# An attention block with its softmax maximum subtracted on VectorE, and three reorderings around it, on one core

## The reference

```python
x = x + tanh(g_xattn) * attention(layernorm(x), ctx, pos, Wq, Wkv, Wout, bout)   # 32 heads of 16
x = x + tanh(g_ffn)   * ffn(layernorm(x), gate_w, w1, w2, shared_w1, shared_w2)

# attention: q = rope(x @ Wq), k = rope(ctx @ Wk), v = ctx @ Wv
#            softmax(q k^T / 4) v, then @ Wout + bout
# ffn:       softmax over 16 experts, the best 6 of each token,
#            each expert and a shared one: (silu(x w1g) * (x w1u)) w2
```

## Time and profile before

| | us |
|---|---|
| median of 3 runs (1628.78 to 1642.08) | 1639.48 |
| the profiled execution | 1645.52 |
| its span, first to last instruction | 1643.7 |
| PE busy (matmul) | 1531.2 |
| DVE busy | 674.6 |
| ACT busy | 563.9 |
| POOL busy | 674.2 |

### The profile page before, as it was taken

One profiled execution on the slowest core, in us unless ns is written; L12 is line 12 of the kernel. 1 busy time (PEld: TensorE's weight loads), 2 busy tenths in 40 slices (PEclk: granted clock), 3 DMA queues, 4 the chain that ended last, 5 costly groups with the idle time before them and its releaser, 6 DMA issues.

```text
span 1643.7 us, 32751 instructions
## 1 busy us (share of the span) xinstructions
PE 1531.2 (93%) x9026; PEld 1296.5 (79%) x9027; DVE 674.6 (41%) x1527; ACT 563.9 (34%) x1370; POOL 674.2 (41%) x1135
## 2 busy tenths in 40 slices
PE   3997999999999873999999999999999999899998
PEld 2675667676666652999999999999999999788887
DVE  4466655555655442222222222222222222245555
ACT  3454555555554520222222222222222222211111
POOL 4436644343444223327344444444444400744442
PEclk9798979888877865999999999999999999999999
DMA  4102332221222114333333333333333232355553
GB/s 174 70 30 69 126 98 104 68 68 68 78 101 85 60 65 172 132 130 130 131 131 134 132 132 135 131 130 130 131 130 115 94 135 81 112 187 173 173 173 116
DMA packets 76313, 190.56 MB, mean 116 GB/s; under 512 B 10497, under 2 KB 12546, under 8 KB 73570
## 3 DMA queue, kind: packets, MB, share of 16 engines
q1 hardware_dynamic: 54562, 99.81, 18.7%
q0 software_dynamic: 21696, 90.06, 15.6%
HBM read 117.07 MB, written 72.76 MB: 115 GB/s over the span
## 4 chain that ended last, share of the span: by engine, by line
PE 57%; issue 1%; DVE 1%; another core or an unknown queue 1%; POOL 1%; DMA 0%; ACT 0%; SPq 0%; DVEq 0%
PE bank L1334 33%; PE bank L1364 18%; PE bank L1305 3%; PE bank L1345 3%; POOL w_lo L209 0%; DVE tree L1429 0%; POOL w_hi L205 0%; DMA xr<-expert_rows 0%; DVE comb L1434 0%; DVE tree L1431 0%; DVE tree L1432 0%; ACT silu L1277 0%; DVE x_lo L1402 0%; DVE a_lo L1408 0%
## 5 line engine op out<-in xcount | busy, mean ns | idle before, releaser
L1334 PE MATMUL bank<-w_hi,x_hi 128*128 (+1 forms) x1152 | 291.7, 334 | 1.6 <-POOL w_lo L209 1.6
L1334 PE MATMUL bank<-w_hi,x_lo 128*128 (+1 forms) x1152 | 279.7, 324 | 0.0
L1334 PE MATMUL bank<-w_lo,x_hi 128*128 (+1 forms) x1152 | 279.7, 324 | 0.0
L205 POOL CAST w_hi<-w_raw 128x352 fp32r<-128x352 f32 x144 | 62.5, 483 | 458.1 <-PE bank L1334 458.1
L1277 ACT ACTIVATE silu<-bank 128x352 f32<-128x352 f32 x144 | 67.0, 465 | 468.6 <-PE bank L1334 454.4
L525 ACT ACTIVATE soft<-bank,smax 128x128 f32<-128x128 f32 x512 | 146.6, 372 | 190.4 <-DVE smax L884 190.1
L1334 PEld LDWEIGHTS bank<-w_hi,x_lo 128*128 128x128 f32 x1152 | 201.6, 188 | 0.0
L1334 PEld LDWEIGHTS bank<-w_lo,x_hi 128*128 128x128 f32 x1152 | 201.6, 188 | 0.0
L1420 DVE SCALAR_TENSOR_TENSOR act<-silu,row_w,bank 128x352 f32<-128x352 f32 x112 | 65.0, 580 | 323.5 <-ACT silu L1277 306.7
L1334 PEld LDWEIGHTS bank<-w_hi,x_hi 128*128 128x128 f32 x1152 | 194.6, 189 | 1.8 <-POOL w_lo L209 1.8
L1364 PE MATMUL bank<-w_hi,a_hi 128*128 (+3 forms) x432 | 172.9, 400 | 13.3 <-DVE a_lo L1408 7.3
(11 more groups left out here) (184 smaller groups left out, 2427.2 us busy)
## 6 DMA issues: line engine op xcount, KB each, us to landing
xr<-expert_rows SPq DMA_DIRECT2D x112, 264.0 KB
y_rows<-y SPq DMA_DIRECT2D x112, 256.0 KB, 2.0
w_raw<-in_w POOLq DMA_DIRECT2D x18, 1408.0 KB, 6.9
w_raw<-in_w POOLq DMA_DIRECT2D x18, 512.0 KB, 8.0
x_sb<-in_x SPq DMA_DIRECT2D x16, 256.0 KB
x_res<-in_x SPq DMA_DIRECT2D x16, 256.0 KB
x_rows<-x SPq DMA_DIRECT2D x16, 256.0 KB
x_rows<-row SPq DMA_DIRECT2D x16, 256.0 KB
```

Source lines behind the costliest of these rows:

```text
L1334: last = nc.tensor.matmul(to[:, 0:WIDTH], xx[jt][:, d, :], w[d][half][:, cols], start=(d == 0 and xx is x_hi and w is w1_hi), stop=(d == D ...
```

## The change

- The block of part A ends without the drain of GpSimd (`no_gpsimd_drain=True`); GpSimd's program of part B begins with a wait for the 96 scatters instead.
- Softmax: DVE subtracts the four maxima from the scores, from PSUM into `soft` in SBUF (128x512, the maxima broadcast along 128 columns), in place of the multiplication of the 128x4 maxima; ACT has one exponential of 512 columns over `soft` in place, with an immediate scale, in place of four with a bias. The score bank is free once DVE has subtracted.
- Projections: V moves from unit 3 to unit 6 (behind `probs`), the transposition of k from unit 6 to unit 5 (behind `probs`); ACT's copies of k move from unit 7 to unit 5, the copy of V from unit 3 to unit 7, `c_hi` from unit 4 to 7; DVE's `c_lo` from unit 5 to 7.
- Part B: `combine` and `finish` of each shared tile stand one step later, its two results alternate between banks 5 and 4, and PE waits for the shared weights only at the first shared tile.

```diff
-        block = st.enter_context(nc.Block())
+        block = st.enter_context(nc.Block(no_gpsimd_drain=True))
...
                     act.wait_ge(shifted, b * GROUPS + u + 1)
-                    need(act, prob_mm, b * GROUPS + u - 1)
-                    for h in range(4):
-                        last = a.activation(soft[u % 2][:, h, :], bank[2 + u % 2][:, h * P:(h + 1) * P], ACT.Exp,
-                                            bias=smax[u % 2][:, h:h + 1], scale=SCALE)
-                    last.then_inc(exp_done, 1)
+                    a.activation(soft[u % 2][:], soft[u % 2][:], ACT.Exp, scale=SCALE).then_inc(exp_done, 1)
...
                     if at(PROJECT) and u == 7:
                         b, j, n = at(PROJECT)
+                        act.wait_ge(v_mm, b + 1)
+                        need(act, pv_mm, (b - 1) * GROUPS)
+                        act.wait_ge(ones_done, 2)
+                        a.activation(v_one[j][:, :, 0:HD], bank[0][:].rearrange("p (h d) -> p h d", h=HEADS),
+                                     ACT.Copy).then_inc(v_done, 1)
+                    attend(at, u)
+                    if at(PROJECT) and u == 5:
+                        b, j, n = at(PROJECT)
                         act.wait_ge(kt_mm, b + 1)
...
-                    attend(at, u)
...
-                    if at(LOAD) and u == 4:
+                    if at(LOAD) and u == 7:
...
-                    need(pe, exp_done, b * GROUPS + u - 1)
+                    need(pe, shifted, b * GROUPS + u - 1)
...
-                    need(pe, kt_done, 2 * b)
+                    need(pe, v_done, b)
...
-                if u == 3:
-                    pe.wait_ge(k_rot, 2 * (b + 1))
-                    three(bank[0][:], ct, kv_w, CC, lambda t, c: t[:, c, :], lambda w, c: w[:, c, D:2 * D])\
-                        .then_inc(v_mm, 1)
                 if u == 4:
                     pe.wait_ge(q_rope_done, b + 1)
-                    pe.wait_ge(v_done, b + 1)
+                    pe.wait_ge(k_rot, 2 * (b + 1))
                     four_transposes(bank[0], q_rope).then_inc(qt_mm, 1)
-                if u == 6:
+
+            def project_late(u, b, j, n):
+                if u == 5:
                     pe.wait_ge(k_rope_done, b + 1)
                     pe.wait_ge(qt_done, b + 1)
                     four_transposes(bank[0], k_rope).then_inc(kt_mm, 1)
+                if u == 6:
+                    pe.wait_ge(kt_done, 2 * (b + 1))
+                    three(bank[0][:], ct, kv_w, CC, lambda t, c: t[:, c, :], lambda w, c: w[:, c, D:2 * D])\
+                        .then_inc(v_mm, 1)
...
-                if u == 5:
+                if u == 7:
                     dve.wait_ge(c_hi_done, b + 1)
...
-                need(dve, exp_done, b * GROUPS + u - 1)
                 v.tensor_reduce(smax[u % 2][:], s3, AX.X, ALU.max).then_inc(smax_done, 1)
                 dve.wait_ge(smax_done, b * GROUPS + u + 1)
-                v.tensor_scalar(smax[u % 2][:], smax[u % 2][:], -SCALE, None, ALU.mult).then_inc(shifted, 1)
+                need(dve, prob_mm, b * GROUPS + u - 1)
+                v.tensor_tensor(soft[u % 2][:], s3, smax[u % 2][:, :, None].to_broadcast([P, 4, P]), ALU.subtract)\
+                    .then_inc(shifted, 1)
...
+        y_banks = (bank[5], bank[4])
...
+        finish_at = {min(BLOCKS + SHARED * (b + 1) + 2, STEPS + 1): b for b in range(BATCHES)}
...
+            for k in range(2):
+                pool.wait_ge(scattered[k], 16 * TOPK * BATCHES // 2)
...
-                    pe.wait_ge(w1_made, 8 * (EXPERTS + s + 1))
+                    if t == BLOCKS:
+                        pe.wait_ge(w1_made, 8 * (EXPERTS + s + 1))
...
-                if first:
+                if routed(i, -2):
                     need(pe, y_done, t)
+                elif first:
+                    need(pe, y_done, t - 1)
...
-                if i is not None and i - 3 >= BLOCKS and ends_tile(i, -2):
-                    finish(tile_of(i - 2) - BLOCKS)
+                if i is not None and i in finish_at:
+                    finish(finish_at[i])
...
-                if i is not None and i - 2 >= BLOCKS and (i - 2 - BLOCKS) % SHARED == 0:
-                    combine((i - 2 - BLOCKS) // SHARED)
+                if i is not None and i + 1 in finish_at:
+                    combine(finish_at[i + 1])
```

More of the change, by code:

```diff
@@ L579, in one_round @@
                         first_work(u)
-                    if at(PROJECT):
-                        b, j, n = at(PROJECT)
-                        if u == 3:
-                            act.wait_ge(v_mm, b + 1)
-                            need(act, pv_mm, (b - 1) * GROUPS)
-                            act.wait_ge(ones_done, 2)
-                            a.activation(v_one[j][:, :, 0:HD], bank[0][:].rearrange("p (h d) -> p h d", h=HEADS),
-                                         ACT.Copy).then_inc(v_done, 1)
                     if at(LOAD) and isinstance(at(LOAD)[0], int) and at(LOAD)[0] == 0 and u == 5:
                         split_weights("q")
-                    if at(LOAD) and u == 4:
+                    if at(LOAD) and u == 7:
                         b, j, n = at(LOAD)
@@ L771, in one_round @@
                         gate_logits(*at(PLACE))
+                    if at(PROJECT):
+                        project_late(u, *at(PROJECT))
                     if at(PLACE) and u == 6:
@@ L1207, in one_step @@
                     load_x1((i - BLOCKS) // 2 + 1)
-                if i is not None and i - 3 >= BLOCKS and ends_tile(i, -2):
-                    b = tile_of(i - 2) - BLOCKS
+                if i is not None and i in finish_at:
+                    b = finish_at[i]
                     sp.wait_ge(y_done, BLOCKS + b + 1)
@@ L1356, in down @@
                     cols = slice(s * D, (s + 1) * D)
-                    pe.wait_ge(w2_made, 3 * (EXPERTS + s + 1))
+                    if t == BLOCKS:
+                        pe.wait_ge(w2_made, 3 * (EXPERTS + s + 1))
                     first, final = s == 0, s == SHARED - 1
                 pe.wait_ge(a_lo_done, g + 1)
-                if first:
+                if routed(i, -2):
                     need(pe, y_done, t)
+                elif first:
+                    need(pe, y_done, t - 1)
+                to = y_bank if routed(i, -2) else y_banks[(t - BLOCKS) % 2]
                 for c, (_, m) in enumerate(WC):
                     for k, (l, w) in enumerate(((a_hi, w2_hi), (a_hi, w2_lo), (a_lo, w2_hi))):
-                        last = nc.tensor.matmul(y_bank[:], l[j][0:m, c, :], w[c][0:m, cols],
+                        last = nc.tensor.matmul(to[:], l[j][0:m, c, :], w[c][0:m, cols],
                                                 start=(first and c == 0 and k == 0),
@@ L1440, in finish @@
                 need(dve, o_out[j], 16 * (b // 2))
-                v.tensor_tensor(o_t[j][:], y_bank[:], comb[j][:], ALU.add).then_inc(y_done, 1)
+                v.tensor_tensor(o_t[j][:], y_banks[j][:], comb[j][:], ALU.add).then_inc(y_done, 1)
             dve.wait_ge(table_in, 16)
```

## The result

The changed kernel took 1624.84 us (median of 10 runs, 1620.15 to 1633.0) beside 1639.66 us of the kernel before in the same measurement: a ratio of 0.9911, 95% interval 0.9885 to 0.9938, so 15 us faster. Forecast were 1618 us and -21. Ratios leave out the slower runs of either kernel, so they can differ a little from the quotient of two medians.

A forecast was written before the change was run, and what follows sets the result against it. PE was taken as the bound, in part A by its work and 6.1 us a round of low clock. Drain and shared tiles -12, moved projections with the clock -9: -21 us from 1639.5 to 1618, range 1585 to 1655.

The forecast's parts named there:

- rival 1: Part A: new waits and the clock cancel at 8 us low time, round unchanged; 1627 us in all, chance 0.22.
- The drain: Passage from part A to part B: going without GpSimd's drain takes 5.0 us off, bounds 0 and 7.
- The shared tiles: Part B: later combining brings -7 us at the first combination, -2 over later tiles, +2 at the end.
- one step later the gathers have landed: -7 us: First combination in part B: moved one step, some 6.5 us, it no longer waits for its gathers, -7 us.
- equal within 0.05 us: Softmax in part A: a group's chain from scores to probabilities takes as long with subtraction and one exponential as before.
- part 3: The softmax change in part A: DVE gains 0.52 us per group, ACT gets 0.5 us more room, chain length equal.
- part 4: The moved projections in part A: +2.1 us of waits, less low clock; -0.6 us a round, -9 over 15 rounds.
- 6.8 us a round: Part A: forecast time at the low clock after the change, in place of 12.2; bounds 3.4 and 13.4.
- rival 3: Part A: moving V cuts nearly every long clock fall, low time 3.4, round 33.5; 1593 us, chance 0.22.
- a fall behind the new 1.6 us of waits in unit 6: Part A, unit 6: the clock falls after PE's waits of 0.45 and 1.15 us and returns soon behind V.
- a dense group: Part A, kernel before: dense matmuls end the short clock falls there; the one of 13.35 us ended only within Q.
- the fall stands 0.05 us behind a wait of 0.58 us: Part A, kernel before: PE's 0.58 us wait for group 6's probabilities precedes the clock's fall; a fall needed only that.

The follow-up runs named there:

- chip C: Chip of the third follow-up job: the kernel before took 1609.5 us, the changed kernel 1587.87 us, a ratio of 0.9874.
- job B: Second follow-up job, on a chip of its own: the kernel before took 1638.8 us, the changed kernel, run again unchanged, 1623.57 us, ratio 0.9935.
- jobs A and C: First and third follow-up jobs, on two different chips, where the kernel before took 1610.0 and 1609.5 us.
- chip A: Chip of the first follow-up job: the kernel before took 1610.0 us, the change with the old softmax 1581.98 us, ratio 0.9823.

## Why the prediction was right, and where it was not

The time came out at -15 us for -21, inside the range and on the side named. At 1624.8 us it is nearer to rival 1's 1627 than to the forecast's 1618, but rival 1's account (a low time of 8 us a round) is not what the profile shows either. Step by step:

- **The drain**: forecast -5.0, measured -5.5 in the first pair, 15.05 us of PE's wait for 20.27 on the two chips without the unnamed idle times. In every profile with the drain this wait is 20.3 to 20.5 us (but for the run with the split moved there), in every one without it 14.8 to 15.2. Right.
- **The shared tiles**: forecast -7 for the first combination, -2 for the later tiles, +2 for the tail. On chip C the three together came to -6.6, in the first measurement to -0.4. The step that failed there is "one step later the gathers have landed: -7 us": they had, but the late silu took the wait's place. The kernel before has two silus late without a named releaser (5.36 us at 1436.47, 5.50 at 1448.05), the first of them hidden behind the wait for the gathers. The later tiles gave about what was forecast (6.0 us of waits became 3.7; 2.6 us on chip C). The tail cost 2.4 us on chip C, as forecast.
- **The softmax**: the exponential over 512 columns takes 0.631 us for the assumed 0.65, the subtraction 0.691 for 0.69, so the price of each operation was right. The step that failed is "equal within 0.05 us", taken as the price of part 3 by itself. The chain of one group is, but DVE's queue as a whole is half a microsecond later per group, and PE meets that where DVE was late already; the clock then falls in every round. Alone this costs 1.7%. With part 4 it came out near nothing: there PE has V to do before it wants group 6, and `c_lo` is out of DVE's way. The wait for `mask` is gone; which of the two did it is not shown.
- **The hold** was in no step: the group of the scaling has 35.1 us in 128 instructions of 0.17, 13 us too many, as its minimum, median and maximum (170, 170 and 8643 ns) tell. The change took it away: the duration of the subtraction that replaces the scaling never leaves 690 to 693 ns. That it is spared because it reads PSUM is likely and not shown. This is 7 to 10 of the 25 us between the profiles (the interval before it is 2.2 us longer than before), and it made up for what the shared tiles did not give. The Trainium skill bears on it: its page "GPSIMD Engine Reference", section "1. Specifications", says that POOL shares its SBUF interfaces with DVE and contends with DVE's instructions in a two-port mode or with two SBUF inputs. The trace agrees as far as it goes, with 8.64 us beside POOL's casts and subtractions, to the end of these. It does not show which mode the scaling, with one SBUF input, ran in.
- **The moved projections**: the layout held but for one wait of 0.45 us that did not come. On chip C, without the unnamed idle times, a pair of rounds takes 64.10 us at full clock, 32.05 a round, where the sum had 29.7 + 2.1 = 31.8. But that agreement is luck, for the sum errs twice and the errors cancel: a round of the kernel before at full clock takes 30.8, not 29.7 (the low level costs 5.0 us a round, not 6.1), and part 4 with part 3 adds 1.2, not 2.1. The low time, "6.8 us a round", measured 3.4 in the first profile (a mean clock of 0.95 for the forecast 0.90) and nothing in most rounds of chip C, as in rival 3. Its mechanism failed too: "a fall behind the new 1.6 us of waits in unit 6" is not there, and the falls that are stand in unit 3. Nor did "a dense group" end all short falls of the kernel before: the one of 6.80 us ends at 423.85, before Q starts at 424.65. Steady rounds were -1.0 on average for the forecast -0.6, -11.1 over eleven.
- **The clock's cause**: the step "the fall stands 0.05 us behind a wait of 0.58 us", read as cause, is refuted as it stood. The same wait stands in rounds at full clock (353.78) and in rounds in which it falls (419.76). So no single wait of this size is enough, nor is one needed: some falls on chips A and C have none near them. The changed kernel's two rounds of 68.22 us have 0.9 us for `ot` and a fall each, those of 64.10 have neither; but every fourth round of the same profile falls at the same place without that wait. The wait for `ot` may make the fall more frequent; that is not shown, for the two profiles are of different measurements. The regimes' cause stays open. The Trainium skill's page "TensorE: Matmul & The Clock Gate", section "HAM oscillation — how this bites in real kernels", ties falls to idle gaps longer than any in the steady rounds. The trace does not agree there: the falls come in rounds whose longest idle time of PE is 0.58 us before and 0.98 after. The one long wait in part A, 9.14 us at 150.09, does have the low clock behind it (the products at 151.43 take 0.63 us).

The gain is near the forecast one, from other sources: the clock a little more, the hold unforeseen, the shared tiles hardly at all in the first measurement. Where DVE and ACT have no such unnamed idle times, the ratio was 0.9874 for 0.9911; the intervals overlap.

## What to carry to other kernels

Read minimum, median and maximum of an instruction whose mean is above its neighbours': one held instruction can be a tenth of what a change is to bring. Price an added operation by the engine's queue at its latest place, not by the chain of its own group, and try the parts of a change alone: here one part lost 1.7%, and beside another it cost next to nothing. Where the clock steps down in some rounds and not in others with equal waits, measure a round in both regimes before putting a price on a wait.

## What the runs showed of the hardware

- A 128x4 scaling on DVE, SBUF to SBUF, took 6.98, 8.64, 11.18 and twice 11.21 us in five profiles (the kernel before twice, the three versions of the change with the old softmax) while POOL ran the second expert's split, and at most 0.97 us when that split ran elsewhere. In the changed kernel the reductions and subtractions that read PSUM, and the statistics of `x_sb`, were not held beside the same split; queued behind a held scaling, three instructions that read PSUM were (recorded with 8.05 to 9.73 us in the change without the softmax, all ending with it).
- In the first measurement and in job B DVE and ACT were idle for up to 4.3 and 9.5 us without any event that the profile names (21 to 39 us in sum on DVE in part A), in the kernel before as in the changed one; in jobs A and C no profile has one above 0.4 us, but for a single one of 3.6 us ahead of `xn` in the first rounds of every kernel with part 4, on all chips. The packets of the instruction queues are few and alike (53 in the changed kernel's profiles of the first measurement and of job C); late instructions would fit, and nothing here shows it.
- The same kernel (before) ran its rounds at 30.8 or at 35.8 us with much the same waits of PE, at a mean granted clock of 1.00 or 0.83.
- The granted clock fell to 0.50 with PE's last wait 0.46 us long and 6.5 us back (changed kernel, chip C, 304.70), and with no wait in the 14 us before (change without the softmax, chip A, 341.53); it stayed at 1.00 behind a wait of 0.98 us (changed kernel, 436.02).
